# The 32x32 block transposition of a query tile: one instruction of 1792 columns or two of 896

## The chip, the cores and the metric

One core of one Trainium2 chip. The metric is the device time of one execution in microseconds (us). The kernel before ran three times: 691.11, 691.82 and 695.0 us, median 691.82 us.

## The reference

Cross attention of 512 query rows over 6250 keys (8 heads of width 64), then an output projection, a layer norm, a feed-forward network and a second layer norm, all in float32:

```python
q  = (M @ Wq.T)                       # 512 x 512, 8 heads of 64
k, v = split(x @ Wkv.T + bkv)         # 6250 keys, 8 heads of 64
sim  = where(mask, q k^T / 8, -1e9)   # per head, 512 x 6250
attn = softmax(sim)
out  = (attn @ v) @ Wo.T + bo
m = layer_norm(out + M)
z = layer_norm(relu(m @ W1.T + b1) @ W2.T + b2 + m)
```

## The kernel before, in words

The keys are cut into 7 chunks of 896. Within a chunk the 8 heads go in 4 pairs, and the 512 queries in 4 tiles of 128 rows. So there are 28 (chunk, pair) rounds of 4 tiles, 112 tiles in all, each with two heads. The running maximum and sum of the softmax are kept between chunks.

One tile passes through the engines so:

- **S on TensorE (L876)**: 12 matmuls fill one PSUM slot for each of the two heads, 128 queries x 896 keys. There are three slots, in a ring.
- **S on VectorE (L721)**: for each head one instruction of 896 columns reads the slot, adds the mask, writes `prob` and, by a short accumulator read, the row's extreme value `negmax`. It frees the slot (`drained`). `prob` has two buffers, used by tile parity, each with both heads.
- **E on ScalarE (L567)**: the exponential of `prob`, in place, one instruction for each head; each raises `exp_done`.
- **X on VectorE (L731)**: one STREAM_TRANSPOSE transposes the 32x32 blocks of both heads, 1792 columns, from `prob` into `st`. It waits until both exponentials of the tile are done (L730) and, on the first tile of a half round, until the DMAs that read the old `st` have landed. It raises `xposed` by one.
- **M on the sync queue (SP, L376) and B on ScalarE's queue (L618)**: after every second tile, 12 DMAs by SP and 4 by ScalarE move the blocks of `st` to their partitions in `pt`. Both wait for `xposed` of the second tile (L372, L614).
- **W on TensorE (L920)**: 7 steps for each round multiply `pt` with the values. Between them TensorE also makes the next keys (K, L802), values (V, L802) and small transposes (F, L929).
- **C, F, A**: ScalarE copies the product out (L597), TensorE transposes it and VectorE adds it to `acc` (L738).

The order on every engine is written out by hand as a table of words for each tile, for example `'S E0 E1 Z K H L X B1'`. X of a tile always comes one tile later than its S. So VectorE executes S(t) for both heads, then X(t-1), then S(t+1) for both heads, then X(t), with an A now and then ahead of an X. S(t+1) writes the `prob` buffer that X(t-1) has just read. That is why its first head waits for `xposed` (L718); the second head waits for nothing of the kind, since it stands behind the first. The value waited for is `QT*n + i - 1`, the count of transpositions up to X(t-1), which is the VectorE instruction directly in front. In the chunk loop such values are computed in registers.

Chunks 0, 1 and 6 are written out; chunks 2 to 5 run as two turns of a hardware loop with two chunks in its body. After the chunks come the projection (L834), the norms (L753 to L757) and the feed-forward loop (L973, L981).

Of the kernel before, what the change touches and what calls it, by code (L numbers as in the profile page):

```python
# [21 lines left out]
QT = E // P  # L22
PAIRS = HEADS // 2
U = 2 * QT
# [16 lines left out]
QUAD = 4  # L41
LANES = P // QUAD
# [93 lines left out]
def build(nc, x, mask, mt, mn, wq, wk, wv, bk, bv, wo, bo, w1, b1, w2, b2, out):  # L136
    with ExitStack() as ctx:
        def sb(name, shape, dt, where=ctx):
            return where.enter_context(nc.sbuf_tensor(name, shape, dt))
# [4 lines left out]
        def sem(name):  # L144
            return ctx.enter_context(nc.semaphore(name))
# [34 lines left out]
        prob = sb("prob", [P, 2, 2, CHUNK], F32, att)  # L180
        st = sb("st", [P, 2, QUAD, 2 * KT, 2 * LANES], F32, att)
# [53 lines left out]
        exp_done = sem("exp_done")  # L235
        xposed = sem("xposed")
# [19 lines left out]
        def in_register(eng, value):  # L256
            return value if isinstance(value, int) else eng.to_reg(value)
# [20 lines left out]
        def is_past(n, bound):  # L278
            return not isinstance(n, int) or n >= bound
# [62 lines left out]
        def _(sp):  # L342
# [16 lines left out]
            def body(c, sched, parity):  # L359
                for kind, p, i in sched:  # L360
                    if kind == "M":
                        n, buf = pair_no(c, p), move_buf(p, i)
                        read = in_register(sp, KT * (n - 1)) if is_past(n, 2) else None
                        written = in_register(sp, QT * n + 2 * i + 2)
                        sp.wait_ge(wv_lo, 1)
                        if isinstance(n, int) and n == 0:
                            sp.wait_ge(wk_lo, 2)
                        if isinstance(n, int) and n < 2:
                            sp.wait_ge(q_filled, PAIRS if n else 1)
                        if read is not None:  # L370
                            sp.wait_ge(pv_done, read)
                        sp.wait_ge(xposed, written)  # L372
                        for turn in (0, 1, 2):
                            for a in (0, 2, 1, 3):
                                b = (a + turn) % QUAD
                                sp.dma_start(pt[LANES * b:LANES * b + LANES, buf, a],  # L376
                                             st[LANES * a:LANES * a + LANES, i, b]).then_inc(landed[buf], 16)
                    if kind == "R":
                        taken = in_register(sp, x_taken(c) + i)
                        sp.wait_ge(zeroed, 2)  # L380
                        sp.wait_ge(xhi_ready, taken)
                        sp.wait_ge(xlo_ready, taken)
                        src = x[c + 1] if isinstance(c, int) else x[bass.ds(c + 1, 1)].rearrange("a p k n -> (a p) k n")
                        sp.dma_start(x_raw[:], src[:, :, i * HALF:i * HALF + HALF]).then_inc(x_in, 16)
                    if kind == "Q":
                        lowered = in_register(sp, (c + 1) * QT)
                        sp.wait_ge(zeroed, 2)
                        sp.wait_ge(lower_ready, lowered)
                        src = mask[c + 1] if isinstance(c, int) else mask[bass.ds(c + 1, 1)].rearrange("a p k n -> (a p) k n")
                        sp.dma_start(mask_raw[:], src).then_inc(mask_in, 16)  # L390
                    if kind == "I" and i == 0:
                        sp.wait_ge(filled[KEYS_RING], keys_use(pair_no(c, PAIRS - 1)) + 1)
                        sp.wait_ge(v_filled, KT * CHUNKS)
                        sp.wait_ge(lower_ready, CHUNKS * QT)
                        sp.wait_ge(klo_done, PAIRS * CHUNKS - 1)
                        sp.dma_start(wo_raw[:], wo).then_inc(wo_in, 16)
                    if kind == "I" and i == 1:
                        sp.dma_start(m_res[:], mn).then_inc(mres_in, 16)
                        sp.wait_ge(pv_done, KT * PAIRS * (CHUNKS - 1))
                        sp.dma_start(bo_sb[:], bo.to_broadcast([P, DM])).then_inc(bias_in, 16)  # L400
                        sp.dma_start(b2_sb[:], b2.to_broadcast([P, DM])).then_inc(bias_in, 16)
                        for j in range(2):
                            sp.dma_start(w1_raw[:, j], w1[j]).then_inc(w1_in[j], 16)
                            sp.dma_start(w2_raw[:, j], w2[j]).then_inc(w2_in[j], 16)
# [127 lines left out]
        def _(act):  # L532
# [26 lines left out]
            def body(c, sched, parity):  # L559
                for kind, p, i in sched:  # L560
                    n = pair_no(c, p)
                    if kind == "E":
                        t, h = i
# [38 lines left out]
                    if kind == "B":  # L602
                        buf = move_buf(p, i)
                        read = in_register(act, KT * (n - 1)) if is_past(n, 2) else None
                        written = in_register(act, QT * n + 2 * i + 2)
                        act.wait_ge(zeroed, 2)
                        if isinstance(n, int) and n == 0:
                            act.wait_ge(wv_lo, 1)
                            act.wait_ge(wk_lo, 2)
                        if isinstance(n, int) and n < 2:  # L610
                            act.wait_ge(q_filled, PAIRS if n else 1)
                        if read is not None:
                            act.wait_ge(pv_done, read)
                        act.wait_ge(xposed, written)  # L614
                        for turn in (3,):
                            for a in (0, 2, 1, 3):
                                b = (a + turn) % QUAD
                                act.dma_start(pt[LANES * b:LANES * b + LANES, buf, a],  # L618
                                              st[LANES * a:LANES * a + LANES, i, b]).then_inc(landed[buf], 16)
# [50 lines left out]
        def _(dve):  # L670
# [28 lines left out]
            def body(c, sched, parity):  # L699
                final = isinstance(c, int) and c == CHUNKS - 1  # L700
                for kind, p, i in sched:
                    n = pair_no(c, p)
                    if kind == "S":
                        masks = taken = None
                        if p == 0 and (i == 0 or not final):
                            masks = in_register(dve, CHUNKS * QT + 1 if final else c * QT + i + 1)
                        if i == 0 and is_past(n, PAIRS):
                            taken = in_register(dve, 2 * (n - PAIRS + 1))
                        free = in_register(dve, QT * n + i - 1) if is_past(QT * n + i, 2) else None
                        for h in range(2):  # L710
                            j, before = unit_use(c, p, i, h)
                            written, u = in_register(dve, before + 1), QT * h + i
                            dve.wait_ge(zeroed, 2)
                            if h == 0 and free is not None:
                                dve.wait_ge(xposed, free)
                            if h == 0 and masks is not None:
                                dve.wait_ge(lower_ready, masks)
                            if h == 0 and taken is not None:  # L718
                                dve.wait_ge(stats_kept, taken)
                            dve.wait_ge(filled[j], written)  # L720
                            nc.vector.tensor_tensor_reduce(  # L721
                                out=prob[:, i % 2, h].rearrange("p (b n) -> p b n", b=2),
                                in0=slot[:, j, :, :HALF], in1=lower[:, i].rearrange("p (b n) -> p b n", b=2),
                                scale=1.0, scalar=negmax_old[:, p, u:u + 1], op0=ALU.add, op1=ALU.min,
                                accum_out=negmax[:, p, u:u + 1]).then_inc(drained[j], 1)
                    if kind == "X":
                        g, t2 = i // 2, i % 2
                        if t2 == 0 and is_past(n, 1):
                            dve.wait_ge(landed[move_buf(p - 1, g)], PAIR_LANDED * moves(c, p - 1))
                        dve.wait_ge(exp_done, U * n + 2 * i + 2)  # L730
                        nc.vector.transpose(  # L731
                            st[:, g].rearrange("p b k (t i) -> p k b t i", t=2)[:, :, :, t2],
                            prob[:, i % 2].rearrange("p h (k b i) -> p (h k) b i", b=QUAD, i=LANES)).then_inc(xposed, 1)
                    if kind == "A":
                        dve.wait_ge(acc_scaled, n + 1)
                        dve.wait_ge(f_filled, n + 1)
# [308 lines left out]
```

## Time and profile before

| | |
|---|---|
| median of 3 runs | 691.82 us (691.11 to 695.0) |
| the profiled execution's own time | 695.23 us |
| its span, first to last instruction | 693.1 us |
| TensorE busy | 635.1 us, 92% |
| VectorE busy | 549.6 us, 79% |
| ScalarE busy | 363.5 us, 52% |
| GpSimd busy | 254.5 us, 37% |
| mean granted TensorE clock | 0.975 |

Busy time of VectorE and ScalarE is that of the instructions alone; waits on semaphores are not in it. The ends of matmuls are modelled. The attention part lasts from about 20 to 555 us of the span. A chunk takes the time from one addition of a round to the same addition of the next chunk, 77.9 us in the loop.

### The profile page before, as it was taken

Reading aid. Unit: us, or ns where it says so; the run is one execution under the profiler, and the core shown is the slowest. Engines: PE = TensorE matmul, PEld = TensorE weight load, DVE = VectorE, ACT = ScalarE, POOL = GpSimd, SP = SyncE. Lnnn points to the kernel's source line nnn. Section 1 sums busy time; section 2 is a strip of 40 time slices with the busy share of each in tenths; the row PEclk is TensorE's granted clock in tenths of the full one; section 3 lists DMA queues with packets and bytes.
Section 4 is the critical chain, followed back from the end, with each engine's and each line's share of the span. In section 5 each row is a group of like instructions: output and inputs, shape, how many; then the busy total and the mean of one; then the engine's idle time right before and its main releaser. Section 6 shows DMA issues by size and latency. Waiting matters only on the chain.

```text
span 693.1 us, 11140 instructions
## 1 busy us (share of the span) xinstructions
PE 635.1 (92%) x3382; PEld 398.1 (57%) x3382; DVE 549.6 (79%) x685; ACT 363.5 (52%) x659; POOL 254.5 (37%) x312
## 2 busy tenths in 40 slices
PE   4899999899999999998999999999998796999994
PEld 3666455555665555655555565545653344788883
DVE  3779999989998999898998999899998726333334
ACT  4566555655655665554665555656564313333322
POOL 3541642265224532263225522363212405422223
PEclk9899999999999999999999999999999799799998
DMA  8058888979898888887887989889786981032221
GB/s 286 3 150 216 226 219 219 238 177 221 220 238 200 221 211 236 211 205 193 210 232 192 216 209 248 210 200 219 189 203 177 256 238 65 30 110 101 91 61 61
DMA packets 56105, 128.36 MB, mean 185 GB/s; under 512 B 15856, under 2 KB 20976, under 8 KB 55792
## 3 DMA queue, kind: packets, MB, share of 16 engines
q1 hardware_dynamic: 45296, 101.97, 57.4%
q10 hardware_dynamic: 10752, 25.70, 14.3%
q8 instruction: 27, 0.44, 0.3%
q14 instruction: 30, 0.25, 0.1%
HBM read 23.80 MB, written 1.05 MB: 36 GB/s over the span
## 4 chain that ended last, share of the span: by engine, by line
PE 48%; DVE 17%; SPq 12%; issue 8%; DMA 5%; ACT 4%; POOL 2%; ACTq 2%; DVEq 1%; POOLq 0%
PE tail L920 12%; SPq L376 11%; PE slot L876 10%; DVE st L731 9%; PE slot L973 6%; PE slot L981 6%; PE tail L802 5%; PE slot L802 5%; DVE prob L721 5%; DMA pt<-st 3%; ACT prob L567 2%; ACTq L618 2%; PE tail L929 2%; DMA wq_raw<-in_wq 1%; PE slot L834 1%
## 5 line engine op out<-in xcount | busy, mean ns | idle before, releaser
L567 ACT ACTIVATE prob<-prob,negmax 128x896 f32<-128x896 f32 x224 | 233.5, 1043 | 206.8 <-DVE negmax L721 191.7
L721 DVE CUSTOM_DVE_ANT_0 prob<-slot,lower,negmax_old 128x896 f32<-128x896 f32 x224 | 249.0, 1149 | 41.9 <-PE slot L876 29.7
L731 DVE STREAM_TRANSPOSE st<-prob 128x1792 f32<-128x1792 f32 x112 | 228.6, 2041 | 6.2 <-DMA pt<-st 5.9
L920 PE MATMUL tail<-pt,val 128*64 128x512 f32 x784 | 186.9, 613 | 7.8 <-ACT outT_sb L597 5.4
L920 PEld LDWEIGHTS tail<-pt,val 128*64 128x64 f32 x784 | 52.8, 139 | 103.8 <-issue 94.8
L876 PE MATMUL slot<-k_hi,q_hi 64*128 64x448 f32 x448 | 95.8, 418 | 13.0 <-DVE negmax L721 6.8
L876 PEld LDWEIGHTS slot<-k_hi,q_hi 64*128 64x128 f32 x448 | 43.8, 185 | 80.8 <-issue 68.9
L876 PE MATMUL slot<-k_hi,q_lo 64*128 64x448 f32 x448 | 84.8, 366 | 0.0
L876 PE MATMUL slot<-k_lo,q_hi 64*128 64x448 f32 x448 | 84.4, 365 | 0.0
L456 POOL TENSOR_TENSOR total<-total,alpha 128x8 f32<-128x8 f32 x28 | 5.8, 206 | 195.4 <-ACT alpha L622 195.3
L477 POOL TENSOR_TENSOR k_lo<-k_raw,k_hi 128x896 fp32r<-128x896 f32 x27 | 57.1, 2114 | 3.9
L431 POOL TENSOR_SCALAR lower<-mask_raw 128x896 bf16<-128x896 uint8 x28 | 27.1, 969 | 52.7 <-DVE negmax L721 41.4
L876 PEld LDWEIGHTS slot<-k_hi,q_lo 64*128 64x128 f32 x448 | 44.4, 187 | 2.7
L512 POOL TENSOR_TENSOR hid_lo<-hid,hid_hi 128x512 fp32r<-128x512 f32 x16 | 21.3, 1332 | 66.5 <-DVE hid_hi L786 66.5
L876 PEld LDWEIGHTS slot<-k_lo,q_hi 64*128 64x128 f32 x448 | 44.5, 188 | 1.2
L802 PE MATMUL tail<-wv_hi,x_hi 128*128 128x512 f32 x98 | 35.9, 447 | 9.2 <-ACT val L576 9.2
L567 ACT ACTIVATION_READ_ACCUMULATOR prob<-prob,negmax 128x1 f32 x224 | 41.8, 186 | 0.0
L802 PE MATMUL slot<-x_hi,wk_hi 128*128 128x448 f32 x112 | 34.0, 386 | 8.0 <-ACT x_hi L542 8.0
L786 DVE CAST hid_hi<-hid 128x512 fp32r<-128x512 f32 x16 | 6.8, 428 | 36.2 <-ACT hid L657 36.2
L802 PE MATMUL slot<-x_lo,wk_hi 128*128 128x448 f32 x112 | 33.0, 377 | 0.0
L802 PE MATMUL slot<-x_hi,wk_lo 128*128 128x448 f32 x112 | 32.9, 376 | 0.0
L657 ACT ACTIVATE hid<-slot,b_sb 128x512 f32<-128x512 f32 x16 | 11.0, 688 | 37.6 <-PE slot L973 37.6
(117 smaller groups left out, 836.6 us busy)
## 6 DMA issues: line engine op xcount, KB each, us to landing
pt<-st SPq DMA_DIRECT2D x672, 112.0 KB, 3.1
pt<-st ACTq DMA_DIRECT2D x224, 112.0 KB, 3.4
w_raw<-in_w SPq DMA_DIRECT2D x32, 256.0 KB, 2.8
x_raw<-in_x SPq DMA_DIRECT2D x13, 448.0 KB, 4.1
mask_raw<-in_mask SPq DMA_DIRECT2D x7, 448.0 KB, 4.3
mt_raw<-in_mt SPq DMA_DIRECT2D x2, 512.0 KB, 8.2
wo_raw<-in_wo SPq DMA_DIRECT2D x1, 1024.0 KB, 7.4
m_res<-in_mn SPq DMA_DIRECT2D x1, 1024.0 KB, 5.1
```

Source lines behind the costliest of these rows:

```text
L376: sp.dma_start(pt[LANES * b:LANES * b + LANES, buf, a], st[LANES * a:LANES * a + LANES, i, b]).then_inc(landed[buf], 16)
L431: nc.gpsimd.tensor_scalar(lower[:, t], mask_raw[:, t], -1.0, -BIG, ALU.add, ALU.mult).then_inc(lower_ready, 1)
L477: nc.gpsimd.tensor_tensor(kst[1][:, p % 2], k_raw[:], kst[0][:, p % 2], ALU.subtract).then_inc(klo_done, 1)
L512: nc.gpsimd.tensor_tensor(hid2[1][:, j], hid[:, j], hid2[0][:, j], ALU.subtract).then_inc(hidlo, 1)
L567: nc.scalar.activation(unit, unit, ACT.Exp, bias=negmax[:, p, u:u + 1], scale=-1.0, accum_out=psumrow[:, p, u:u + 1]).then_inc(exp_done, 1)
L721: nc.vector.tensor_tensor_reduce(out=prob[:, i % 2, h].rearrange("p (b n) -> p b n", b=2), in0=slot[:, j, :, :HALF], in1=lower[:, i].rearr ...
L731: nc.vector.transpose(st[:, g].rearrange("p b k (t i) -> p k b t i", t=2)[:, :, :, t2], prob[:, i % 2].rearrange("p h (k b i) -> p (h k) b ...
L802: last = nc.tensor.matmul(dst, stationary(a, k), moving(b, k), start=(n == 0), stop=(n == len(terms) - 1))
L876: last = nc.tensor.matmul(slot[:, j, b, :HALF], q2[qa][rows(h), p, P * i:P * i + P], key_half(p, b, kb)[rows(h)], start=(part == 0), stop= ...
L920: last = nc.tensor.matmul(outT[DH * h:DH * h + DH], val[:, val_at(i, parity ^ (p < 0)), head(p, h)], moving, start=(i == 0), stop=(i == KT ...
L973: last = nc.tensor.matmul(slot[:, 2, j], w12[a][:, j, k], mT2[b][:, k], start=(i == 0), stop=(i == len(terms) - 1))
L981: last = nc.tensor.matmul(slot[:, t // 2, t % 2], hid2[a][:, j, P * t:P * t + P], w22[b][:, j], start=first and i == 0, stop=last_one and ...
```

## The change

X becomes two transpositions of 896 columns, one for each head. Each waits for the exponential of its own head and raises `xposed`, so a tile raises it by two. S of each head waits for the transposition of the same head two tiles earlier, in place of one wait ahead of the first head. SP and ScalarE wait for doubled counts (the first lines of the diff are SP's; ScalarE's in B are the same).

```diff
-    written = in_register(sp, QT * n + 2 * i + 2)
+    written = in_register(sp, 2 * (QT * n + 2 * i + 2))
...
-    free = in_register(dve, QT * n + i - 1) if is_past(QT * n + i, 2) else None
     for h in range(2):
         j, before = unit_use(c, p, i, h)
         written, u = in_register(dve, before + 1), QT * h + i
+        free = in_register(dve, 2 * (QT * n + i - 2) + h + 1) if is_past(QT * n + i, 2) else None
         dve.wait_ge(zeroed, 2)
-        if h == 0 and free is not None:
+        if free is not None:
             dve.wait_ge(xposed, free)
...
-    dve.wait_ge(exp_done, U * n + 2 * i + 2)
-    nc.vector.transpose(
-        st[:, g].rearrange("p b k (t i) -> p k b t i", t=2)[:, :, :, t2],
-        prob[:, i % 2].rearrange("p h (k b i) -> p (h k) b i", b=QUAD, i=LANES)).then_inc(xposed, 1)
+    for h in range(2):
+        dve.wait_ge(exp_done, U * n + 2 * i + h + 1)
+        nc.vector.transpose(
+            st[:, g].rearrange("p b (h k) (t i) -> p h k b t i", h=2, t=2)[:, h, :, :, t2],
+            prob[:, i % 2, h].rearrange("p (k b i) -> p k b i", b=QUAD, i=LANES)).then_inc(xposed, 1)
```

## Rows read from the trace of the kernel before

**Rows 1.** Windows: busy time of each engine in one chunk of the loop

```profile
core 0: us, PE busy (x) PEld busy (x) DVE busy (x) ACT busy (x) POOL busy (x), PEclk, DMA share, GB/s
294.73:372.61 77.88, 73.61 (x412) 44.40 (x410) 69.65 (x85) 44.21 (x83) 28.96 (x37) 0.98 0.83 207
```

**Rows 2.** Waits, 59 to 550 us: who waited, for whom, us in total, times, longest

```profile
DVE prob L721 <- PE slot L876: 21.5, 32, 1.3
DVE st L731 <- DMA pt<-st: 2.3, 5, 1.1
DVE prob L721 <- DVE st L731: 1.1, 3, 0.5
DVE st L731 <- ACT prob L567: 0.2, 1, 0.2
...
PE slot L876 <- DVE negmax L721: 5.5, 7, 2.0
```

**Rows 3.** The chain that ended last, 59 to 555 us, shares by line

```profile
by line: PE tail L920 15.3%; SPq L376 14.8%; PE slot L876 12.7%; DVE st L731 12.0%; issue 10.0%; DVE prob L721 6.3%; PE tail L802 6.1%; PE slot L802 5.9%; DMA pt<-st 4.8%; ACT prob L567 2.4%; PE tail L929 2.2%; ACTq L618 1.6%; DVE acc L738 
```

**Rows 4.** VectorE timeline: start us, us, instruction; first and last of 69 undisturbed passes

```profile
49.68 2.04 DVE L731 STREAM_TRANSPOSE st<-prob 128x1792 f32<-128x1792 f32 x1 [0.49 <-DMA pt<-st]
51.85 1.15 DVE L721 CUSTOM_DVE_ANT_0 prob<-slot,lower,negmax_old 128x896 f32<-128x896 f32 x1
...
542.86 2.04 DVE L731 STREAM_TRANSPOSE st<-prob 128x1792 f32<-128x1792 f32 x1
545.03 1.15 DVE L721 CUSTOM_DVE_ANT_0 prob<-slot,lower,negmax_old 128x896 f32<-128x896 f32 x1
```

**Rows 5.** VectorE timeline, last chunk: a transposition, then an addition that doesn't wait for it

```profile
550.37 2.05 DVE L731 STREAM_TRANSPOSE st<-prob 128x1792 f32<-128x1792 f32 x1 [3.11 <-DMA pt<-st]
552.34 0.65 DVE L738 TENSOR_TENSOR acc<-acc,tail 128x512 f32<-128x512 f32 x1
```

**Rows 6.** VectorE timeline, preamble: one operation at 512 and at 1536 columns

```profile
10.68 0.69 DVE L683 TENSOR_TENSOR wq_lo<-wq_raw,wq_hi 128x512 fp32r<-128x512 f32 x1 [1.61 <-ACT wq_hi L544]
...
18.53 1.75 DVE L695 TENSOR_TENSOR wq_lo<-wq_raw,wq_hi 128x1536 fp32r<-128x1536 f32 x1
```

**Rows 7.** Chain in order of time (start us, us): first and last of 23 passes X to S

```profile
59.03 1.97 DVE st L731
61.00 0.04 DVEq L720
61.03 0.09 issue
61.12 0.11 DVE prob L721
...
504.22 1.97 DVE st L731
506.18 0.04 DVEq L720
506.22 0.09 issue
506.30 0.11 DVE prob L721
```

**Rows 8.** Chain in order of time: one of 5 passes from X to the sync queue

```profile
336.99 1.97 DVE st L731
338.96 0.02 issue
338.98 0.03 SPq L372
339.00 0.03 issue
339.03 0.53 SPq L376
```

**Rows 9.** Windows: the stretch behind the loop's turn, granted clock in column PEclk

```profile
320.00:327.00 7.00, 6.76 (x28) 4.15 (x28) 5.12 (x6) 1.32 (x3) 1.16 (x3) 0.76 0.81 200
```

**Rows 10.** Chain in order of time: TensorE's groups ahead of, in and behind that stretch

```profile
302.86 3.65 PE tail L920 x16
...
320.24 2.60 PE slot L876 x12
322.84 4.28 PE tail L920 x16
327.12 1.43 PE slot L876 x11
```

More of the change, by code:

```diff
@@ L604, in body @@
                         read = in_register(act, KT * (n - 1)) if is_past(n, 2) else None
-                        written = in_register(act, QT * n + 2 * i + 2)
+                        written = in_register(act, 2 * (QT * n + 2 * i + 2))
                         act.wait_ge(zeroed, 2)
```

## The prediction

> **What bounds the kernel now.** I read the windows first, then the waits, then the chain. The windows show one chunk of the loop: of 77.88 us TensorE is busy for 73.61 and VectorE for 69.65 [rows 1], so neither is idle for long and TensorE is the fuller. The waits say who holds whom. Over the attention part VectorE sat idle 21.5 us for a slot that TensorE had not filled, in 32 places, and TensorE only 5.5 us for a slot that VectorE had not drained; VectorE hardly ever waited for an exponential (0.2 us) [rows 2]. The chain of waits splits the same stretch by line: the four big TensorE lines have 40%, SP's issues of the block moves 14.8%, the transposition 12.0% and S on VectorE 6.3% plus a part of the "issue" share [rows 3]. So VectorE is on the chain in turns with TensorE and the sync queue. A faster VectorE is worth something only in its turns.
>
> The change touches the place between X and the next S. A transposition takes 2.04 us, and in 69 of the passes the next S starts 2.16 to 2.18 us after it started [rows 4]. That is later than the end of the transposition, because this S writes the buffer X has read and waits for its semaphore. In one place, in the last chunk, an addition that doesn't wait for X stands behind it; it starts 1.97 us after X did, before X is through [rows 5]. The wait thus costs 2.17 - 1.97 = 0.20 us for each X.
>
> **Part 1: the wait ahead of S.** After the change S of head 0 waits for the first half of X only, which ended long before (the second half lies between), and S of head 1 waits for the second half, which ends while S of head 0 runs. That S lasts 1.15 us, more than the 0.13 by which S now follows the end of X [rows 4]. The wait's 0.20 us go. Nothing new is late on VectorE: the extra register value and the extra wait are handled while an instruction of about 1 us runs, so I cost them at nothing. If that cover is gone they cost 0.04 us for a satisfied wait, and 0.09 for the step behind it [rows 7].
>
> **Part 2: one instruction more for each X.** The trace has no transposition of 896 columns. Its price comes from the column rate: 512 columns take 0.69 us and 1536 take 1.75 [rows 6], or 1.035 ns a column, so 896 columns less are 0.93 us less. A half X lasts 2.04 - 0.93 = 1.11 us, and an instruction that isn't held starts 1.97 - 0.93 = 1.04 us behind it. Two halves and the S behind: 2 x 1.04 = 2.08 us, against 2.17 now. **Gain: 0.09 us for each X that S follows at once.** This supposes that a transposition may start under the tail of another as the addition did. No row shows that. The bounds: at best the second half pays no fixed part and the pass takes 1.97 us (gain 0.20); at worst it is held as S is now, and starts 1.11 + 0.13 = 1.24 us behind the first, so that the pass takes 2.28 us (loss 0.11). I take 0.09 since its two steps have the form of the row of the addition, in which the wait is satisfied before.
>
> A rule speaks against the gain. The Trainium skill, "VectorE: DVE Perf Modes", section "The DRAIN you can't avoid", says that the next operation does not start until the pipeline has emptied, that a semaphore between two operations costs nothing more, and that one should save instructions and not semaphores. Here the addition started 0.07 us before the transposition ended [rows 5], against the first half of this; whether it holds between two transpositions no run here shows. By it a pass would take at least 2 x 1.11 = 2.22 us and lose 0.05. The same skill's "Vector Engine (DVE) Microarchitecture Reference", section "Measured stream behaviour on trn2", gives about 75 ns for each instruction after overlap; an estimate by that page is 2 x (0.93 + 0.075) = 2.01 us for the pass, a gain of 0.16 in place of 0.09.
>
> **Part 3: the end of X.** The pair of halves ends 1.04 + 1.11 = 2.15 us after its start, 0.11 later than now. SP and ScalarE start their moves on that end. On the chain this matters in 5 passes from X to SP [rows 8]. The doubled counts add no instruction to their queues: 12 moves of SP and 4 of ScalarE for each half round stay as they are. That head 0 need not wait for the exponential of head 1 saves at most the 0.2 us of [rows 2].
>
> **The sum.** On the chain X is followed by S in 23 passes [rows 7]: 23 x 0.09 = 2.1 us gained. The 5 others cost 5 x 0.11 = 0.6 us. Net -1.5 us, against the profiled execution's own 695.23 us (span 693.1): 693.7. That execution is 3.4 us above the median of the three runs, 691.82; by the median I forecast **690.3 us**. The other passes are off the chain: there VectorE comes earlier to a wait for TensorE, of which it has 21.5 us already. A measurement of this kernel tells about 0.5%, 3.5 us, from no change, so this forecast counts as no change.
>
> **Rivals.**
>
> *Faster: the near ties fall too.* The chain shows one path of several that are almost as long. If all 69 undisturbed passes counted in full, the gain would be 69 x 0.09 = 6.2 us: 685.6. It takes about 40 passes for more than 3.5 us, or 23 at a gain of 0.16. For it: VectorE runs for rounds on end without a wait, and part of TensorE's idleness hides in modelled matmul ends. Against: a shorter path can't give more than its passes on the chain unless the order of the work changes, and TensorE has only 4.3 us of slack in a chunk [rows 1].
>
> *Nothing: TensorE takes it all.* VectorE waits for slots as much longer as it got faster: 691.8. For it, 21.5 against 5.5 us [rows 2]. This lies inside the same 0.5%.
>
> *Slower: two transpositions don't overlap.* The place is the step from the first half to the second. The pass loses as soon as this step is over 2.17 - 1.04 = 1.13 us; unheld it is 1.04. If it is 1.24, each of the 23 passes costs 0.11 (2.5 us), and the pair ends 1.24 + 1.11 = 2.35 us after its start, 0.31 later than now, at 5 places (1.6 us): 695.9. With all 69 passes it would be 7.6 + 1.6 = 9.2 us: 701.0. For it: no row has X behind X, and the block transposition may need its store emptied. Against: the addition behind X.
>
> *The clock, either way.* Behind the loop's turn TensorE idled 1.6 us, and the granted clock of that stretch is 0.76, the mean of a part at 1.2 GHz and a part at 2.4 [rows 9]. Twelve S matmuls took 2.60 us there against 1.43 behind it, sixteen W took 4.28 against 3.65 [rows 10]: 1.8 us. Another placement of idle time can bring one such stretch more or less. That widens the range by 1.8 us on both sides and makes no case by itself.
>
> **How the numbers follow.** The forecast and "nothing" are both within 0.5%: 0.45 and 0.15. Faster by near ties or by a cheaper second half: 0.22. Slower by held transpositions: 0.18, nearly all of it beyond 3.5 us. So faster 0.22, same 0.60, slower 0.18. The range goes down to 686.5, the forecast less most of the near ties or less the cheaper half and a clock stretch, and up to 696.0, the first price of the slower rival.
>
> **What would show it.** In the changed profile two transpositions of about 1.11 us should start 1.04 us apart, S should start 2.08 us behind the first, and no S should follow its transposition by more than its end. A chunk of the loop should take 77.6 us or so in place of 77.9; VectorE's idle time for PE slots should grow by some 5 us from 21.5; 224 transpositions should be busy for 249 us in place of 228.6. A step of 1.1 us or more between the halves means the slower rival; a chunk under 77.2 us means the faster one. The prediction is wrong if TensorE waits for VectorE in far more than 7 places, or if S behind X still comes at 2.17.

## The result, and the profile after

Over 7 runs each, the changed kernel takes 687.91 us (686.11 to 689.95) and the kernel before 693.23 us: a ratio of 0.9923, interval 0.9898 to 0.9947, 5.3 us faster. In a second set the same kernel came to 0.994 (0.9917 to 0.9962), 4.2 us at 692.91. So it is a gain of 0.6 to 0.8%, above the 0.5% that a measurement can tell, but not by much; the forecast had been 1.5 us. The profiled execution has a span of 686.6 us, against 693.1 before.

VectorE's timeline of the changed kernel, start us and length us; it answers to [rows 4]:

```profile
297.23 1.15 DVE L721 CUSTOM_DVE_ANT_0 prob<-slot,lower,negmax_old 128x896 f32<-128x896 f32 x1
298.30 0.09 DVE L721 DVE_READ_ACCUMULATOR2_ANT negmax<- 128x1 f32 x1
298.30 2.10 DVE L732 STREAM_TRANSPOSE st<-prob 128x896 f32<-128x896 f32 x2
300.33 1.11 DVE L721 CUSTOM_DVE_ANT_0 prob<-slot,lower,negmax_old 128x896 f32<-128x896 f32 x1
...
301.36 1.15 DVE L721 CUSTOM_DVE_ANT_0 prob<-slot,lower,negmax_old 128x896 f32<-128x896 f32 x1
```

The two halves stand in one merged line: 2.10 us from the start of the first to the end of the second. S starts at 300.33, 2.03 us behind the first half and 0.07 before the second has ended; in 75 of the 110 passes the step is 2.02 or 2.03 us, where 69 had 2.16 to 2.18. The second head's S then starts 1.03 us behind the first (301.36), not 1.07 or 1.08. So an undisturbed tile is 0.15 + 0.03 = 0.18 us shorter, twice the 0.09 forecast.

The windows of two chunks, for the kernel before and for the changed one (columns as in [rows 1]). The first is an ordinary chunk, the second holds the turn of the hardware loop:

```profile
161.27:235.83 74.56, 71.79 (x412) 42.42 (x411) 69.63 (x85) 44.38 (x84) 28.96 (x36) 1.00 0.88 219
296.16:374.05 77.89, 73.61 (x414) 44.40 (x412) 69.66 (x87) 44.23 (x84) 28.97 (x37) 0.98 0.83 207
```

```profile
159.94:233.55 73.61, 71.61 (x412) 42.21 (x411) 69.37 (x101) 44.34 (x84) 28.96 (x36) 1.00 0.87 219
293.57:370.51 76.94, 72.21 (x414) 42.24 (x412) 69.56 (x101) 44.28 (x85) 28.99 (x37) 1.00 0.85 212
```

The chunk of [rows 1] was the odd one: it has the loop's turn in it, and 3.3 us of its length are that. An ordinary chunk took 74.56 us and takes 73.61. Not every chunk gains the 0.95: the six steps from one chunk to the next are 0.2 to 0.95 us shorter, 4.2 us together, and the rest of the 6.5 us by which the spans differ lies ahead of them (0.6) and behind them (1.7). TensorE is busy 1.4 us less in the chunk with the loop's turn, at a granted clock of 1.00 in place of 0.98, so a part of the difference between these two profiles is the clock. VectorE's busy sum did not fall (69.63 and 69.37): what it won lies between instructions, where a busy sum does not look. If all 16 tiles of a chunk win 0.18 us, 2.9 us were won on VectorE, and 0.95 came out.

Waits of the changed kernel, 59 to 550 us, against [rows 2]:

```profile
DVE prob L721 <- PE slot L877: 20.5, 27, 1.2
DVE st L732 <- DMA pt<-st: 11.5, 14, 2.6
...
PE tail L803 <- ACT val L576: 6.6, 6, 1.1
...
PE slot L877 <- DVE negmax L721: 4.6, 8, 2.0
...
PE tail L921 <- ACT outT_sb L597: 4.3, 6, 0.8
```

VectorE now comes early to the landing of the moves: 11.5 us in 14 places, where it had been 2.3 in 5. Its wait for slots did not grow (20.5 against 21.5). On TensorE's side two short waits for ScalarE stand once in each chunk, as they did before (6.8 and 5.4 us in 6 places each); the last experiments come back to them. The chain, 59 to 555 us as in [rows 3], shows the same shift, from VectorE to the moves:

```profile
by line: SPq L376 21.0%; PE tail L921 15.4%; PE slot L877 12.4%; DVE st L732 10.5%; issue 7.1%; PE tail L803 6.5%; DMA pt<-st 5.9%; PE slot L803 5.9%; DVE prob L721 5.7%; ACT prob L567 1.8%; PE tail L930 1.8%; ACTq L618 1.7%; DVE acc L739 1
```

### The profile page after: what moved, and what is told of

Read it like the earlier page. It is cut to its first block, busy times and chain, and to the rows that moved or that the text cites. A ratio compares the mean times of both kernels' runs of the same rounds, so it can differ in the third digit from the quotient of the medians.

```text
span 686.6 us, 11356 instructions
## 1 busy us (share of the span) xinstructions
PE 630.6 (92%) x3382; PEld 394.4 (57%) x3382; DVE 549.4 (80%) x797; ACT 363.7 (53%) x659; POOL 254.5 (37%) x312
## 4 chain that ended last, share of the span: by engine, by line
PE 49%; SPq 16%; DVE 16%; DMA 6%; issue 6%; ACT 3%; ACTq 1%; POOL 1%; DVEq 1%; POOLq 0%
SPq L376 15%; PE tail L921 12%; PE slot L877 11%; DVE st L732 8%; PE slot L974 6%; PE slot L982 6%; PE tail L803 6%; PE slot L803 5%; DMA pt<-st 4%; DVE prob L721 4%; ACT prob L567 2%; DMA wq_raw<-in_wq 1%; PE tail L930 1%; ACTq L618 1%; PE slot L835 1%
## 5 line engine op out<-in xcount | busy, mean ns | idle before, releaser
L721 DVE CUSTOM_DVE_ANT_0 prob<-slot,lower,negmax_old 128x896 f32<-128x896 f32 x224 | 246.2, 1136 | 30.8 <-PE slot L877 28.0
L732 DVE STREAM_TRANSPOSE st<-prob 128x896 f32<-128x896 f32 x224 | 235.3, 1088 | 12.9 <-DMA pt<-st 12.1
L921 PE MATMUL tail<-pt,val 128*64 128x512 f32 x784 | 184.1, 605 | 6.6 <-ACT outT_sb L597 4.3
L921 PEld LDWEIGHTS tail<-pt,val 128*64 128x64 f32 x784 | 51.4, 137 | 102.0 <-issue 95.1
L877 PE MATMUL slot<-k_hi,q_hi 64*128 64x448 f32 x448 | 95.2, 418 | 11.5 <-DVE negmax L721 6.0
L450 POOL TENSOR_TENSOR drop<-negmax,negmax_old 128x8 f32<-128x8 f32 x28 | 5.7, 204 | 67.7 <-ACT prob L567 67.2
```

The lines of the kernel that those rows point to most:

```text
L721: nc.vector.tensor_tensor_reduce(out=prob[:, i % 2, h].rearrange("p (b n) -> p b n", b=2), in0=slot[:, j, :, :HALF], in1=lower[:, i].rearr ...
L732: nc.vector.transpose(st[:, g].rearrange("p b (h k) (t i) -> p h k b t i", h=2, t=2)[:, h, :, :, t2], prob[:, i % 2, h].rearrange("p (k b ...
L877: last = nc.tensor.matmul(slot[:, j, b, :HALF], q2[qa][rows(h), p, P * i:P * i + P], key_half(p, b, kb)[rows(h)], start=(part == 0), stop= ...
L921: last = nc.tensor.matmul(outT[DH * h:DH * h + DH], val[:, val_at(i, parity ^ (p < 0)), head(p, h)], moving, start=(i == 0), stop=(i == KT ...
```

## Experiments

### Is it the wait ahead of S, or the half's own wait for its exponential?

Three kernels part the two. `two_x_wait_both` keeps the two halves and gives S its old wait back:

```diff
-    free = in_register(dve, 2 * (QT * n + i - 2) + h + 1) if is_past(QT * n + i, 2) else None
+    free = in_register(dve, 2 * (QT * n + i - 1)) if h == 0 and is_past(QT * n + i, 2) else None
```

> The changed kernel, but S of head 0 waits for both halves of the transposition in front of it, as S did before the change; the second head has no wait. Theory A (the gain is the wait of S for the VectorE instruction directly in front, which the second half now covers): S starts 1.03 + 1.10 + 0.13 = 2.26 us behind the first half, against 2.02 in the changed kernel and 2.17 before, so the kernel is slower than before by 0.09 us in 25 to 69 passes, 2 to 6 us, ratio 1.003 to 1.009. Theory B (the gain comes from each half waiting for the exponential of its own head, or from smaller instructions as such): about as fast as the changed kernel, ratio 0.992.

Measured: 693.48 us, ratio 1.0022 (1.0004 to 1.004), 1.5 us slower than before by the ratio and 1.2 by the medians. VectorE's timeline:

```profile
300.24 2.10 DVE L732 STREAM_TRANSPOSE st<-prob 128x896 f32<-128x896 f32 x2
302.47 1.15 DVE L721 CUSTOM_DVE_ANT_0 prob<-slot,lower,negmax_old 128x896 f32<-128x896 f32 x1
...
303.54 1.15 DVE L721 CUSTOM_DVE_ANT_0 prob<-slot,lower,negmax_old 128x896 f32<-128x896 f32 x1
```

S now starts 302.47 - 300.24 = 2.23 us behind the first half, 0.13 behind the end of the second, and lasts its full 1.15 us. The split alone costs 0.06 us a tile (2.23 against 2.17); the wait's absence brings 0.21. The loss stayed under the 2 us of the lowest estimate, which had 0.09 us for each pass where 0.06 were measured.

`two_x_exp_both` leaves S as in the changed kernel and lets both halves wait for both exponentials:

```diff
-    dve.wait_ge(exp_done, U * n + 2 * i + h + 1)
+    dve.wait_ge(exp_done, U * n + 2 * i + 2)
```

> The changed kernel, but both halves wait for both exponentials of the tile, as the whole transposition did. Theory A: nothing is lost, since the second exponential was done ahead of the transposition in all but one place (0.2 us); S still starts 2.02 us behind the first half, ratio 0.992 within 0.003. Theory B: the gain is gone, ratio 1.000 within 0.003.

Measured: 688.27 us, ratio 0.9943 (0.9925 to 0.9962). That is the second measurement of the changed kernel (0.994) to within its interval, and the steps from the first half to S are 2.02 and 2.03 us. Waiting for each head's own exponential brings nothing that can be measured.

`one_x_three_prob` has the one wide transposition and takes away what makes S wait, by a third buffer (the lines that store the low halves of wk and wv over the high ones, so that the weights are the low halves alone, are not shown):

```diff
-        prob = sb("prob", [P, 2, 2, CHUNK], F32, att)
+        prob = sb("prob", [P, 3, 2, CHUNK], F32, att)
...
+        PROB_AT = (0, 1, 2) * 4 + (0, 1, 0, 2)      # buffer of each tile of a chunk
...
-                        free = in_register(dve, QT * n + i - 1) if is_past(QT * n + i, 2) else None
+                        free = in_register(dve, QT * n + i - prob_gap(p, i) + 1) if is_past(QT * n + i, prob_gap(p, i)) else None
```

> The kernel before, with one transposition of 1792 columns for each tile, and three prob buffers in place of two, so that in 14 of 16 tiles S writes a buffer whose transposition ended one tile earlier. To make room the low halves of the weights wk and wv are stored over their high halves, with the same instructions, so those weights are only the low halves. Theory A: S starts 1.97 us behind the transposition in those passes, 0.20 earlier than before and 0.05 earlier than in the changed kernel, with no second instruction; ratio 0.992 or a little under (0.988 to 0.993). Theory B: ratio 1.000 within 0.003, since no head's exponential is waited for separately.

Measured: 688.48 us, ratio 0.9946 (0.9924 to 0.9968). VectorE's timeline:

```profile
299.23 2.04 DVE L740 STREAM_TRANSPOSE st<-prob 128x1792 f32<-128x1792 f32 x1
301.19 1.11 DVE L730 CUSTOM_DVE_ANT_0 prob<-slot,lower,negmax_old 128x896 f32<-128x896 f32 x1
...
302.23 1.15 DVE L730 CUSTOM_DVE_ANT_0 prob<-slot,lower,negmax_old 128x896 f32<-128x896 f32 x1
```

S starts 1.96 us behind the wide transposition, before its end, and again 1.04 us ahead of the second S. That holds in 42 passes. In 12 more the step is still 2.17 or 2.18: there S writes one of the two buffers in 16 for which it must still wait. And in 18, each the fourth tile of a round, it is 1.99, with S starting 0.17 us behind the last matmul of its slot, as in nearly all the places where VectorE waits for TensorE (0.15 to 0.18). There the slot was not ready sooner. The ratio is thus no better than that of the changed kernel, where 0.988 to 0.993 had been expected. One instruction with the wait taken away does what two instructions do. Theory A holds in all three: **the gain is that S no longer waits for the instruction directly in front of it.** The split is only the way to put something between the two, and it costs 0.06 us of the 0.21.

### How much does each further instruction cost?

`four_x` cuts the transposition in four, two for each head, by block columns:

```diff
-    nc.vector.transpose(
-        st[:, g].rearrange("p b (h k) (t i) -> p h k b t i", h=2, t=2)[:, h, :, :, t2],
-        prob[:, i % 2, h].rearrange("p (k b i) -> p k b i", b=QUAD, i=LANES)).then_inc(xposed, 1)
+    for s in range(2):
+        part = slice(2 * s, 2 * s + 2)
+        nc.vector.transpose(
+            st[:, g].rearrange("p b (h k) (t i) -> p h k b t i", h=2, t=2)[:, h, :, part, t2],
+            prob[:, i % 2, h].rearrange("p (k b i) -> p k b i", b=QUAD, i=LANES)[:, :, part]).then_inc(xposed, 1)
```

> The changed kernel with four transpositions of 448 columns for each tile, two for each head; S of a head waits for both of that head. If each instruction costs its columns and a fixed 0.10 us, as a step of 1.03 us for 896 columns says, a quarter's step is 0.57 us and S starts 2.26 us behind the first quarter, against 2.02 with halves and 2.17 before: VectorE has 0.24 us more in each tile than with halves, and the kernel comes out at a ratio of 0.998 to 1.008. If the fixed part is smaller for short instructions, the ratio stays under 0.996.

Measured: 692.06 us, ratio 0.999 (0.9968 to 1.0012). The four show as one line (the S behind this group waits for its slot; the steps below are from the passes that don't):

```profile
302.59 2.23 DVE L734 STREAM_TRANSPOSE st<-prob 128x448 f32<-128x448 f32 x4
```

The group lasts 2.22 or 2.23 us against 2.10 for two halves and 2.04 for one whole; S starts 2.14 or 2.15 us behind its first, against 2.02. So two more instructions cost 0.12 to 0.13 us, 0.06 each, not 0.10. The ratio lies in the range that was expected while the size of the step does not. By the sum further down, the later end of the group, on which the moves start, makes up for the cheaper step; no run separates the two.

### A different order of the same instructions

`two_x_between` puts the first half between the two S (the order in words; the edit calls the transposition of a half between them):

```diff
-    order on VectorE: S head 0, S head 1, X head 0, X head 1
+    order on VectorE: S head 0, X head 0, S head 1, X head 1
```

> The changed kernel with VectorE's order S head 0, first half, S head 1, second half, in place of S, S, half, half. Theory A: no S waits for the instruction in front in either order, each step stays at 1.03 to 1.08 us, and VectorE's own work for a tile is the same; ratio near 0.992, within 0.004 either way. It is slower than the changed kernel only if the first half, now one step earlier, waits for the landing of the moves: then VectorE's idle time for DMA grows from 12.1 us by more than 5. If the even draining of slots helps TensorE, its time for VectorE (6.0 us) falls and the ratio is under 0.988.

Measured: 738.84 us, ratio 1.0674 (1.064 to 1.0709). This was expected by no theory. VectorE's steps are 1.03 or 1.04 us for each of the four wherever it does not wait, and its busy sum in a chunk is nearly unchanged (69.68 us), but the chunk takes 81.40 us:

```profile
172.69:254.09 81.40, 73.27 (x410) 42.78 (x410) 69.68 (x101) 45.29 (x83) 28.95 (x36) 0.98 0.82 198
```

The waits, 59 to 550 us:

```profile
DVE prob L740 <- PE slot L894: 45.6, 35, 3.2
PE slot L894 <- DVE negmax L740: 23.7, 17, 2.2
DVE st L705 <- DMA pt<-st: 21.6, 18, 2.4
...
PE tail L820 <- ACT val L576: 10.5, 5, 2.2
```

TensorE waits for VectorE 23.7 us (4.6 in the changed kernel) and VectorE for TensorE 45.6 (20.5 there): both at once, the sign of an order and not of an engine that is too slow. With three slots, S of the third tile needs the slot that head 1 of the second tile drains. In the changed kernel both halves, 2.03 us, lie between that drain and VectorE's next S; in this order only one, 1.03, and TensorE's twelve matmuls take 1.5. One such place:

```profile
272.70 1.11 DVE L740 CUSTOM_DVE_ANT_0 prob<-slot,lower,negmax_old 128x896 f32<-128x896 f32 x1
...
273.87 0.48 PE L894 MATMUL slot<-k_hi,q_hi 64*128 64x448 f32 x2 [1.98 <-DVE negmax L740]
...
275.55 1.15 DVE L740 CUSTOM_DVE_ANT_0 prob<-slot,lower,negmax_old 128x896 f32<-128x896 f32 x1 [0.71 <-PE slot L894]
```

All 17 of TensorE's waits for VectorE stand ahead of the third tile of a round; in the changed kernel one of the 8 does. VectorE's waits grow there too, from 11.1 to 16.3 us, but more on the second tile, from 9.4 to 24.2, and for that the ring gives no reason by itself: it may be what follows from TensorE's lost time. A kernel that changes the ring alone was not run, so the cause is read from the trace and not shown by a run.

### What limits behind the change?

`two_x_768` leaves 128 of 896 columns out of each half (by the expectation 4.3 us less for VectorE in a chunk), `two_x_short_v` a third of the products for V (TensorE), and `one_x_short_v` the same in the kernel before:

```diff
+    kept = slice(0, KT if isinstance(c, int) and c == 0 else KT - 1)      # two_x_768, in both patterns of the transposition
...
-                                 split(DC)).then_inc(v_filled, 1)
+                                 split(DC)[:4]).then_inc(v_filled, 1)      # two_x_short_v and one_x_short_v
```

> The changed kernel, with the last 128 of 896 columns left out of each half of the transposition from the second chunk on (those keys then use what the first chunk left in st). VectorE has 0.13 us less work in each of 192 halves, some 26 us in all, 4.3 us in a chunk; nothing else changes. Theory C (behind the change VectorE is no longer what limits; TensorE or the moves do): the time stays within 3 us of the changed kernel's 688, a chunk at 73.0 to 73.6 us. Theory D (VectorE is still the limit and only the measured gain is small because of the ring of slots): a chunk falls by over 1.5 us and the kernel to 678 or less.

Measured: 687.52 us, ratio 0.9907 (0.9886 to 0.9928). An ordinary chunk is 73.39 us:

```profile
158.01:231.40 73.39, 71.56 (x412) 42.25 (x411) 65.64 (x103) 44.34 (x85) 28.97 (x36) 1.00 0.89 222
```

VectorE is busy 3.7 us less in it (65.64 against 69.37), and the chunk is 0.2 us shorter. It waits for slots 36.8 us in place of 20.5. The chunk with the loop's turn went the other way: 80.1 us at a granted clock of 0.96, against 76.9 at 1.00, so the kernel's time alone would hide a part of what the other chunks gained (0.2 to 0.8 us each). Theory C all the same: in an ordinary chunk VectorE has left the bound.

> The changed kernel, with the third of the three products (x_lo times wv_hi) left out of the values V: two of six matmuls for each of 49 steps, 0.53 us each by the chain (1.60 us for six), 26 us of TensorE in all, 3.7 us in a chunk. Theory C with TensorE as the limit: a chunk falls by 2 us or more and the kernel to 675 or less. If the moves (SP's issues and their landing) are the limit: within 4 us of 688.

> The same third product left out of the kernel before. If VectorE was the limit before the change and TensorE after it, this falls less than the changed kernel does: a chunk from 74.4 to 73 or so, the kernel by 5 us or less. If TensorE was already the limit before, both fall by the same 15 to 20 us.

Measured: 681.03 us, ratio 0.9817 (0.9798 to 0.9837), with the change; 687.24 us, ratio 0.9912 (0.9893 to 0.9931), without. Both intervals lie apart from those without the cut: the cut brings some 7 to 8.5 us in the changed kernel (by the ratios 0.9923 and 0.994 without it) and 6 to 7 in the one before. By the profiles TensorE is busy 17 us less in the changed kernel (630.6 to 613.6) and 22 us less in the other (635.1 to 613.5), not the 26 that were expected. So neither clean case of the expectations came. TensorE counts in both, and a second limit lies close behind it: an ordinary chunk with the cut takes 72.41 us with TensorE busy for only 68.54.

```profile
158.38:230.79 72.41, 68.54 (x398) 39.81 (x397) 69.14 (x103) 44.28 (x85) 29.03 (x36) 1.00 0.89 222
```

`two_x_act5` asks whether that is the sync queue, which had grown to 21% of the chain. One of its 12 moves goes to ScalarE's queue:

```diff
+    if (turn, a) == (2, 3):      # in M, on the sync queue
+        continue
...
-    for turn in (3,):            # in B, on ScalarE's queue
+    for turn in (2, 3):          # of turn 2 only a = 3
```

> The changed kernel, with one of the 12 moves of each half round given from the sync queue to ScalarE's queue (11 and 5). The sync queue has 0.64 us less in each half round, 5 us in a chunk, ScalarE as much more. If the sync queue's issues are the limit behind the change (they had 21% of the chain): ratio to before under 0.988. If they are not, ScalarE's added 0.64 us ahead of its exponentials shows: ratio 0.993 to 1.01.

Measured: 691.94 us, ratio 0.9957 (0.9933 to 0.9982), if anything slower than the changed kernel. The sync queue's issues are not a limit that is worth ScalarE's time: it now waits 43.5 us for transpositions (16.8 in the changed kernel), so it has slack. The ordinary chunk stayed at 73.6 us, and the 21% of the chain were time that was nearly free elsewhere.

### Two waits of TensorE, and a version that beats both kernels

In the ordinary chunk of the changed kernel TensorE is busy 71.61 us of 73.61. Most of the rest is two waits, each once in a chunk, both for a copy on ScalarE that stands behind the two exponentials of its tile:

```profile
133.34 0.73 PE L803 MATMUL tail<-wv_hi,x_hi 128*128 128x512 f32 x2 [1.14 <-ACT val L576]
152.54 3.65 PE L921 MATMUL tail<-pt,val 128*64 128x512 f32 x16 [0.81 <-ACT outT_sb L597]
```

Moving each copy between the exponentials is a change of two words in the order table:

```diff
-     'S E0 E1 V4 X B0'),
+     'S E0 V4 E1 X B0'),
...
-     'S E0 E1 W5 W6 C X B0 J1 I'),
+     'S E0 W5 W6 C E1 X B0 J1 I'),
```

> The changed kernel itself, on the chip of the next three, to compare them with it. Ratio 0.992 within 0.003.

> The changed kernel, with two copies of ScalarE moved ahead of an exponential in the hand-written order: the copy C of the last round of a chunk, and the value copy V4 in the second pair. In each chunk TensorE stalls 0.7 to 0.8 us for the one and 1.1 us for the other, and a chunk is as long as TensorE's own work and these two stalls (71.5 + 1.8 = 73.3 us). If TensorE's own chain is the limit behind the change, a chunk falls to between 71.8 and 72.8 us and the kernel by 5 to 11 us against the changed kernel, ratio 0.977 to 0.986. If the moves (issue and landing) are a limit of equal size, it falls by under 3 us.

> The same two moves of ScalarE's copies in the kernel before. There VectorE's own work, 71.5 us in a chunk, is as long as TensorE's. If VectorE is what holds the kernel before, the two stalls of TensorE are mostly covered: less gain than in the changed kernel, ratio 0.993 to 1.000. If TensorE alone held both kernels, the same gain of 5 to 11 us.

Measured on one chip, before at 692.91 us:

| kernel | us | ratio to before (interval) |
|---|---|---|
| two_x_again, the changed kernel | 688.75 | 0.994 (0.9917 to 0.9962) |
| one_x_both_orders | 685.68 | 0.9893 (0.987 to 0.9916) |
| two_x_both_orders | 682.09 | 0.9832 (0.9807 to 0.9857) |

The reordered kernel with halves beats both, by 10.8 us against the kernel before and by 6.7 us against the changed one. The reordering brings 7.2 us without the halves and 6.7 with them, and the halves bring 4.2 us without it and 3.6 with it. In its waits TensorE's wait for the value copy is down to 0.2 us in one place and that of L921 for outT_sb is gone, so TensorE's two stalls are removed, 6.6 + 4.3 = 10.9 us, and 6.7 come out; a part comes back in other waits (for POOL's k_lo 3.2 us in place of 1.1). In the kernel before I had thought it likelier that VectorE covers those stalls (0 to 5 us); the 7.2 us refute that. They fit the other case, TensorE alone, but then the halves should bring nothing on top, and they bring 3.6. So the kernel before is held by TensorE and VectorE in turns, and the two gains add up but for 0.6 us, which is within the intervals.

## Why the prediction was right, and where it was off

The direction and the place were right, and the time lies in the range. But the gain is about three times the forecast, and by my own line of 3.5 us it is the "faster" outcome, to which I gave 0.22, and not "no change". The range reached 5.3 us below the 691.82 of the kernel before, and the measured gain was 5.3, so a part of the success is the width of the range. Its lower end stood for the near ties, or for a cheaper second half with a clock stretch; the cheaper half is what came. The second measurement, 4.2 us, lies well inside.

**What bounds it.** Right in kind: VectorE on the chain in turns, and the place is the step from X to S. Off in two readings: I took the one chunk with the loop's turn for typical [rows 1] and put TensorE's slack at 4.3 us. In an ordinary chunk it was 74.56 - 71.79 = 2.8. And the chain has 25 passes from X to S, not the 23 of [rows 7]: 30 transpositions stand on it, 5 of them ahead of the sync queue.

**Part 1, the wait's price.** Right: 0.20 forecast from one row [rows 5]. The kernels with and without the wait differ by 2.23 - 2.02 = 0.21 with two halves, and by 2.17 - 1.96 = 0.21 with one instruction. The extra register value and wait left no trace in the steps.

**Part 2, the second instruction.** This is the term that was mis-sized. I carried the fixed part of the step in front of the addition, 1.04 - 0.93 = 0.11 us, to both halves: 2.08. Measured 2.02, against 1.96 with one unheld transposition, so a further transposition adds 0.06. Two transpositions do overlap: the second starts 1.03 us behind the first, which is recorded with 1.11, and the S behind it 0.99. The Trainium skill's "VectorE: DVE Perf Modes", section "The DRAIN you can't avoid", was read too narrowly in the prediction. It says that the next operation starts only when the pipeline is empty, but adds that one that is not held starts earlier; the trace agrees with the addition (0.07 us of overlap). Its measurement of copies, in which a semaphore costs nothing more, does not carry over to the wait of S for the instruction directly in front: 0.21 us here. The estimate from the Trainium skill's "Vector Engine (DVE) Microarchitecture Reference", section "Measured stream behaviour on trn2", 2.01 us, was the better one; the trace agrees with it in the sum (2.02), with the two steps at 1.03 and 0.99. Nothing in the sum had the 0.03 us by which the second S comes sooner when the first follows without a wait. These two, 0.06 and 0.03, are the whole of what 0.09 lacked to 0.18.

**Part 3, the end of X.** 0.11 forecast, 0.06 measured (2.10 against 2.04). The 249 us that I gave as a sign for the 224 transpositions are 224 x 1.11, without the overlap that my own step of 1.04 supposes; with it they would have been 112 x 2.15 = 241, and measured were 235.3.

**The sum.** The count from the chain was near, the price was not. With 0.18 us in 23 passes and 0.06 in 5 the same sum gives -4.1 + 0.3 = -3.8 us; with the 25 passes that the chain has, -4.2. Measured were -5.3 and -4.2. The same counts (23 and 5) come near for the other kernels: S held behind two halves, 28 x 0.06 = +1.7 us (measured +1.5); a third buffer, 0.24 us in 7 of 8 of the 23 passes, -4.8 (measured -3.7); four quarters, 23 x (2.14 + 1.04 - 3.24) + 5 x 0.19 = -0.4 (measured -0.7), where 3.24 is the 2.17 + 1.07 of before. With 25 they are +1.8, -5.3 and -0.6. The third buffer gained less than its sum; that in 18 passes the slot comes last explains a part of it. Where the cut is large the sum fails: in `two_x_768` the step can be 1.75 us, 0.42 less than before, with 0.03 more for the second S, which gives over 10 us, and 6.5 came; only 38 passes have that step (1.75 or 1.76), and 23 are at 1.98 or 1.99, with S again 0.17 us behind the last matmul of its slot. A path that gets shorter can't give more than its count on the chain, and less once another is as long.

**The rivals.** The slower one is out, since the halves overlap. "TensorE takes it all" is out for the first 0.18 us and right for what would come behind. The faster one is nearest in size, but not by its mechanism: the gain is by a cheaper pass on the counted passes, and 40 near ties are not needed for it. What the first measurement has beyond the sum, 1.1 to 1.5 us, may be near ties or the clock; no run separates them. I had named that way (a gain of 0.16 in 23 passes) as its second half. Among the signs I gave, the wait for slots did not grow by 5 us (21.5 to 20.5); the wait for the moves' landing grew by 9. The chunk with the loop's turn, 77.6 forecast and under 77.2 as the sign of the faster rival, took 76.94 in the first profile and 77.28 in the second: it does not decide. The clock stayed a width: the chunk with the loop's turn was granted 1.00 in the first of these profiles and 0.98 in the second.

## What to carry to other kernels

Look in the timeline for an instruction that starts later than the end of the one in front, on the same engine, with no other engine to blame: it may wait for its neighbour's semaphore, and that cost 0.21 us each time here. Another buffer takes it away; splitting the neighbour, so that one part stands between, does it too, for 0.06 us. Putting another instruction between the two took it away as well, but changed the order in which slots came free and cost 6.7%. To size it, count the passes on the chain and multiply by the price of one, and before counting on more, shorten that engine far beyond the plan once and see whether the chunk follows.

## What the runs showed of the hardware that was not expected

An S of VectorE that follows a transposition without waiting is recorded with 1.11 us (`after`, `one_x_three_prob`) and the S behind it starts 1.04 us later, against 1.15 and 1.07 when it had to wait. A further transposition costs 0.06 us, at 896 columns and at 448. And an order of VectorE's instructions that left its unheld steps at 1.03 us and its busy sum as it was made the kernel 6.7% slower: TensorE waited 23.7 us for VectorE and VectorE 45.6 us for TensorE, by my reading through the ring of three slots.
